# Attention passes of a graph network: one wide addition of keys and values on VectorE, and every fourth step's values added by GpSimd

## Chip, cores and metric

One core of one Trainium2 chip. The metric is the device time of one execution in microseconds (us). The kernel before takes 4827.84 us, the median of 3 runs (4825.83 to 4828.0).

## What is computed

The reference is a residual network over a graph of 6250 nodes with 256 features and 100000 edges, sorted by destination, each with a source, a weight and 194 attributes. First a weighted sum of neighbours with two products and a layer norm, then two attention layers one after the other, a residual and a layer norm. All is float32. The attention layer, twice:

```python
q, k, v = x @ Wq + bq, x @ Wk + bk, x @ Wv + bv       # [n, 4 heads, 64]
e = edge_attr @ We                                     # [edges, 4, 64]
kj, vj = k[src] + e, v[src] + e
logits = einsum('ehc,ehc->eh', q[dst], kj) / sqrt(64)
a = softmax of logits over the edges of one dst
out = segment_sum(vj * a[:, :, None], dst).reshape(n, 256) + x @ Ws + bs
```

What matters here is the line of `kj` and `vj`: the same edge row `e` is added to the gathered key row and to the gathered value row.

## The kernel before

The edges are cut into tiles of 128. Since a tile may touch two or more blocks of 128 destination nodes, each pair of a tile and a block is a step: there are 832, padded. Both attention layers run `edge_pass_attention` (L1130), called as `e1` at L1596 and `e2` at L1599; between them and around them stand short passes over the 49 blocks of nodes. The first also computes a product per block beside its edges (`skip`), the second doesn't. The loops are unrolled; the order on each engine is as written, and semaphores join the engines.

A step `i` of an attention pass:
- GpSimd gathers, for each of the 128 edges, one row of 512 numbers, key and value side by side, from a table in memory into slot `i % 6` of `kv` (L1303, an indirect DMA). It may do so when VectorE has made the value sum of step `i - 6` (`vj_done`). Once in four steps, ahead of the gather of a step with `i % 4 == 2`, it also makes `pick` for the four steps of that quad (L1294, 128x512): a matrix of ones and zeros with which TensorE copies query rows to edges.
- The edge row: in three steps of four TensorE multiplies the edge attributes by `We` (L1315, L1316) into one of two PSUM banks. In the fourth (`i % 4 == 3`) the row comes from a table in memory that the first pass of the program has made; SyncE loads it into `made`, two buffers, when VectorE is done with the quad two before (L1240).
- TensorE: the query rows of the step's edges (L1325).
- VectorE (`logits`, L1403): the key sum into one of two places of `kvj` (L1416), the value sum into one of 44 further places of the same tile (L1420), then for each head a product with the query row and its sum over 64 columns (L1428, an instruction and the reading of its accumulator).
- Every 26 steps are a batch. VectorE, TensorE and ScalarE turn its logits into weights, in stages laid among the steps of the next batch.
- 42 steps behind (`LAG`), ScalarE makes a mask of the step's destinations (L1561, L1567) and multiplies the values by their weights (L1571), 4 instructions; TensorE multiplies mask and weighed values (L1366); VectorE adds the result to the running sums `acc` (L1510). In the last 42 steps VectorE does part of ScalarE's share (L1515, L1517).

A key place is free when the dot products of two steps before are done. A value place is free when ScalarE has weighed the step 44 before it (`weighed`). GpSimd fills all of `kvj` with ones once per pass (L1296), since the last column of each head must be 1; VectorE waits for that before it starts.

Lines that the change and the prediction touch: the load of `made` (L1240), GpSimd's loop (L1296 to L1305), the wait ahead of the edge product (L1314), VectorE's two additions (L1416, L1420) with their waits, and the two places that read values (L1517, L1571).

Of the kernel before, what the change touches and what calls it, by code (L numbers as in the profile page):

```python
# [7 lines left out]
P = 128  # L8
D = 256
H = 4  # L10
C = D // H
# [4 lines left out]
QUAD = 4  # L16
# [1113 lines left out]
def edge_pass_attention(nc, name, k, t, s, w_edge, edge_rows_made, kv_rows, pens, locals16, singles, skip_of):  # L1130
# [13 lines left out]
    with Phase(nc, name) as ph:  # L1144
# [17 lines left out]
        if skip_of is not None:  # L1162
# [21 lines left out]
        made_got = ph.sems("made_got", 2)  # L1184
        w_got, cleared, ones_set = ph.sem("w_got"), ph.sem("cleared"), ph.sem("ones_set")
        e_done, q_done, kj_done, vj_done, dots_done, picked, apart_done = (
            ph.sem(n) for n in ("e_done", "q_done", "kj_done", "vj_done", "dots_done", "picked", "apart_done"))
# [37 lines left out]
        with nc.Block() as block:  # L1225

            @block.sync
            def _(e):
# [9 lines left out]
                def load_made(c):  # L1238
                    if c >= 2:
                        e.wait_ge(vj_done, (c - 1) * QUAD)  # L1240
                    e.dma_start(made[:, c % 2, :], edge_rows_made[c * P:(c + 1) * P, :]).then_inc(made_got[c % 2], 16)
# [45 lines left out]
            @block.gpsimd  # L1287
            def _(e):
                def pick_rows(c):

                    e.wait_ge(spots_got[c % 2], 16 * (c // 2 + 1))
                    if c >= 2:
                        e.wait_ge(q_done, (c - 1) * QUAD)
                    e.tensor_scalar(pick[:, c % 2, :], spots[:, c % 2, :], k["own"][:, 0:1], None, ALU.is_equal).then_inc(picked, 1)  # L1294

                e.memset(kvj[:], 1.0).then_inc(ones_set, 1)  # L1296
                for i in range(T):
                    u = i % NG
                    if i % QUAD == 2:
                        pick_rows(i // QUAD)  # L1300
                    if i >= NG:
                        e.wait_ge(vj_done, i - NG + 1)
                    e.indirect_dma_start(out=kv[:, u, :], out_offset=None,  # L1303
                                         **rows_of(kv_rows, k["src"][:, i:i + 1])).then_inc(kv_got[u], 16)
                e.wait_ge(ones_set, 1)  # L1305

            @block.tensor
            def _(e):
                chosen = Numbers(e, f"{name}_chosen", k["q_row"], (s.blocks - 1) * D)

                def edge_product(a):
                    e.wait_ge(ea_got[a % NE], 16 * (a // NE + 1))
                    if a >= 2:
                        e.wait_ge(vj_done, step_of(a - 2) + 1)  # L1314
                    e.matmul(pe_e[a % 2][:, 0:D], ea[:, a % NE, 0:P], we[:, 0, :], start=True, stop=False)  # L1315
                    e.matmul(pe_e[a % 2][:, 0:D], ea[:, a % NE, P:2 * P], we[:, 1, :],  # L1316
                             start=False, stop=True).then_inc(e_done, 1)
# [74 lines left out]
            def _(e):  # L1392
# [10 lines left out]
                def logits(i):  # L1403
                    j, r = i // BATCH, i % BATCH + 1
                    e.wait_ge(kv_got[i % NG], 16 * (i // NG + 1))
                    c, at = i // QUAD, i % QUAD
# [7 lines left out]
                    if i >= 2:  # L1414
                        e.wait_ge(dots_done, i - 1)
                    e.tensor_tensor(kvj[:, i % 2, :, 0:C], kv[:, i % NG, 0:D].rearrange("p (h c) -> p h c", h=H), edge,  # L1416
                                    ALU.add).then_inc(kj_done, 1)
                    if i >= NV:
                        e.wait_ge(weighed, i - NV + 1)
                    e.tensor_tensor(kvj[:, 2 + i % NV, :, 0:C], kv[:, i % NG, D:].rearrange("p (h c) -> p h c", h=H), edge,  # L1420
                                    ALU.add).then_inc(vj_done, 1)
                    e.wait_ge(kj_done, i + 1)
# [89 lines left out]
                def late_part(n):  # L1512
# [3 lines left out]
                    e.wait_ge(ex_done, b + 1)  # L1516
                    e.tensor_scalar(vals[:, n % R, h * HV:(h + 1) * HV], kvj[:, 2 + n % NV, h, :], ex[:, b % 2, h, r:r + 1], None,  # L1517
# [18 lines left out]
            def _(e):  # L1536
                for i in range(END):
# [18 lines left out]
                    if 0 <= n < T:  # L1556
# [12 lines left out]
                        e.wait_ge(ex_done, b + 1)  # L1569
                        for h in range(H if n < LATE else H - 1):  # L1570
# [83 lines left out]
```

## Time and profile before

| what | us |
|---|---|
| median of 3 runs | 4827.84 |
| profiled execution, device time | 4832.06 |
| its span, first to last instruction | 4830.3 |
| VectorE busy | 3989.0 |
| TensorE matmul busy | 4189.2 |
| ScalarE busy | 2982.2 |
| GpSimd busy | 3116.4 |

Two stretches of the span, 1365 to 2950 us and 3126 to 4690 us, are the two attention passes. Before them lie the making of index tables and the pass of weighted sums. Busy times are unions over an engine's instructions and say nothing yet on who waits for whom; where one instruction's row overlaps the next one's, the distance from start to start is what it costs. The time that an engine is not busy before an instruction is printed with what ended it; "issue" there means that nothing which the profile shows was waited for.

### The profile page before, as it was taken

The page shows a single profiled execution, that of the slowest core. Times are in us where ns is not written, and L with a number is a line of the kernel's source. Part 1 is how long each engine was busy: PE and PEld are TensorE (multiplying, and loading weights), DVE is VectorE, ACT ScalarE, POOL GpSimd, SP SyncE. Part 2 cuts the span into 40 slices and gives each one's busy share as a digit, 9 for nine tenths or more (in the row PEclk, how much of TensorE's full clock was granted, in tenths as well). Part 3 has the DMA queues.
Part 4 walks back from the last instruction along what each step waited for, and adds up shares of the span by engine and source line. Part 5 has one row for each costly group of instructions (what it writes and reads, how often), then busy time and mean ns, then how long its engine had stood idle before and what let it go on. Part 6 is the DMA issues. An engine that isn't in the chain of part 4 may idle for free. (4 is left out here: it accounts for less than half of the span.)

```text
span 4830.3 us, 107746 instructions
## 1 busy us (share of the span) xinstructions
PE 4189.2 (87%) x17694; PEld 3210.6 (66%) x17694; DVE 3989.0 (83%) x22772; ACT 2982.2 (62%) x10607; POOL 3116.4 (65%) x2996
## 2 busy tenths in 40 slices
PE   2887887888979999999999998889999999999988
PEld 2766666675547777777777774567777777777755
DVE  4655555556869999999999998789999999999986
ACT  1111111112319898989898984149999999989971
POOL 6677777740067777777777771287777777777730
PEclk9999999999999999999999999999999999999989
DMA  4666666654568887878788773587777777777734
GB/s 121 189 192 196 192 193 193 191 167 149 169 212 237 233 236 232 233 229 236 231 234 228 231 230 104 173 247 231 226 230 228 231 228 227 226 228 231 226 114 149
DMA packets 663064, 996.73 MB, mean 206 GB/s; under 512 B 99667, under 2 KB 489690, under 8 KB 662407
## 3 DMA queue, kind: packets, MB, share of 16 engines
q0 software_dynamic: 171408, 540.40, 38.1%
q1 hardware_dynamic: 491000, 449.44, 30.8%
q14 instruction: 471, 3.86, 0.3%
q8 instruction: 185, 3.03, 0.3%
HBM read 870.01 MB, written 119.44 MB: 205 GB/s over the span
## 5 line engine op out<-in xcount | busy, mean ns | idle before, releaser
L1303 POOL DMA_INDIRECT e_kv<-kv,src x1664 | 1635.0, 983 | 748.1 <-DVE e_kvj L1420 449.7
L1571 ACT ACTIVATE e_vals<-e_kvj,e_ex 128x65 f32<-128x65 f32 x6572 | 1725.1, 334 | 5.5 <-PE e_sum L1366 5.1
L1366 PE MATMUL e_sum<-e_vals,e_mask 128*128 128x260 f32 x3328 | 1063.7, 403 | 206.2 <-ACT e_vals L1571 190.0
L1325 PE MATMUL e_q<-q,e_pick 128*128 x3328 | 1017.2, 387 | 95.3 <-DVE e_logit L1428 66.4
L1428 DVE CUSTOM_DVE_ANT_0 e_kvj<-e_kvj,e_q 128x64 f32<-128x64 f32 x6656 | 1060.2, 214 | 3.4 <-PE e_q L1325 2.2
L152 POOL DMA_INDIRECT e_x<-x_rows,e_src x783 | 747.3, 954 | 263.1 <-issue 172.3
L1366 PEld LDWEIGHTS e_sum<-e_vals,e_mask 128*128 128x128 f32 x3328 | 563.0, 190 | 454.4 <-issue 379.7
L1325 PEld LDWEIGHTS e_q<-q,e_pick 128*128 128x128 f32 x3328 | 618.2, 191 | 252.4 <-issue 169.9
L1315 PE MATMUL e_e<-e_we,e_ea 112*128 112x256 f32 x2496 | 752.3, 382 | 17.4 <-DMA e_ea<-attr_tiles 16.2
L1316 PE MATMUL e_e<-e_we,e_ea 112*128 112x256 f32 x2496 | 745.8, 380 | 0.0
L1510 DVE TENSOR_TENSOR acc<-acc,e_sum 128x260 f32 x1664 | 697.3, 419 | 41.4 <-issue 23.6
L530 ACT ACTIVATE q<-e_edges 128x512 f32<-128x512 f32 x208 | 124.2, 597 | 925.5 <-PE e_edges L523 921.7
L1294 POOL TENSOR_SCALAR e_pick<-e_spots,own 128x512 f32<-128x512 bf16 x416 | 660.9, 1589 | 15.4 <-DMA e_spots<-locals 1.1
L1567 ACT ACTIVATE e_mask<-e_apart,one 128x128 f32<-128x128 f32 x1580 | 634.6, 402 | 52.5
L597 PE MATMUL e_sum<-e_x,e_mask 128*128 x1664 | 455.2, 400 | 210.6 <-DVE e_mask L612 114.0
L620 DVE TENSOR_TENSOR acc<-acc,e_sum 128x256 f32 x832 | 349.9, 421 | 332.0 <-PE e_sum L597 308.0
L1561 ACT ACTIVATE e_apart<-iota,local 128x128 f32<-128x128 f32 x1580 | 610.4, 386 | 0.0
L1416 DVE TENSOR_TENSOR e_kvj<-e_kv,e_e 128x256 f32<-128x256 f32 x1248 | 513.4, 411 | 66.2 <-DMA e_kv<-kv,src 40.3
L1315 PEld LDWEIGHTS e_e<-e_we,e_ea 112*128 112x128 f32 x2496 | 477.7, 192 | 96.4 <-issue 20.3
L1420 DVE TENSOR_TENSOR e_kvj<-e_kv,e_e 128x256 f32<-128x256 f32 x1248 | 514.7, 412 | 21.0 <-ACT e_vals L1571 20.6
L1428 DVE DVE_READ_ACCUMULATOR2_ANT e_logit<- 128x1 f32 x6656 | 531.6, 80 | 0.2 <-issue 0.2
L597 PEld LDWEIGHTS e_sum<-e_x,e_mask 128*128 128x128 f32 x1664 | 316.9, 198 | 312.2 <-issue 270.2
(223 smaller groups left out, 4479.1 us busy)
## 6 DMA issues: line engine op xcount, KB each, us to landing
e_ea<-attr_tiles SPq DMA_DIRECT2D x1248, 112.0 KB
edges<-q SPq DMA_DIRECT2D x208, 256.0 KB
e_spots<-locals SPq DMA_DIRECT2D x416, 128.0 KB
e_made<-edges SPq DMA_DIRECT2D x416, 128.0 KB
e_kv<-kv,src POOLq DMA_INDIRECT x1664
kv<-n_proj_rows SPq DMA_DIRECT2D x98, 256.0 KB
q<-attr_tiles SPq DMA_DIRECT2D x208, 112.0 KB
n_x<-x_rows SPq DMA_DIRECT2D x98, 128.0 KB
```

What stands on the lines that cost most here:

```text
L152: e.indirect_dma_start(out=self.x[:, at:at + D], out_offset=None, **rows_of(self.t["x_rows"], self.src[:, i:i + 1])).then_inc(self.got[i / ...
L597: e.matmul(sums[i % SUMS][:, 0:D], mask[:, i % R, :], rows, start=True, stop=True).then_inc(summed, 1)
L1294: e.tensor_scalar(pick[:, c % 2, :], spots[:, c % 2, :], k["own"][:, 0:1], None, ALU.is_equal).then_inc(picked, 1)
L1303: e.indirect_dma_start(out=kv[:, u, :], out_offset=None, **rows_of(kv_rows, k["src"][:, i:i + 1])).then_inc(kv_got[u], 16)
L1315: e.matmul(pe_e[a % 2][:, 0:D], ea[:, a % NE, 0:P], we[:, 0, :], start=True, stop=False)
L1316: e.matmul(pe_e[a % 2][:, 0:D], ea[:, a % NE, P:2 * P], we[:, 1, :], start=False, stop=True).then_inc(e_done, 1)
L1325: e.matmul(pe_q[i % 2][:, 0:D], pick[:, c, at:at + P], rows, start=True, stop=True).then_inc(q_done, 1)
L1366: e.matmul(sums[n % 2][:, 0:VALS], mask[:, n % R, :], vals[:, n % R, :], start=True, stop=True).then_inc(summed, 1)
L1428: dot = e.tensor_tensor_reduce(kvj[:, i % 2, h, 0:C], kvj[:, i % 2, h, 0:C], pe_q[i % 2][:, hs], 1.0, 0.0, ALU.mult, ALU.add, logit[:, j % ...
L1510: e.tensor_tensor(rows, rows, sums[n % 2][:, 0:VALS], ALU.add).then_inc(added, 1)
L1567: e.activation(mask[:, n % R, :], apart[:], ACT.Relu, bias=k["one"][:, 0:1], scale=-1.0).then_inc(masked, 1)
L1571: by_weight = e.activation(vals[:, n % R, h * HV:(h + 1) * HV], kvj[:, 2 + n % NV, h, :], ACT.Copy, scale=ex[:, b % 2, h, r:r + 1])
```

## The change

The key sum and the value sum of a step become one VectorE instruction of 512 columns, in three steps of four. It writes to two places of `kvj`, and reads the edge row twice. In the fourth step VectorE makes the key sum alone, and GpSimd makes the value sum from `kv` and `made`, right behind the gather that lies four steps ahead. One semaphore, `kvj_done`, takes the part of `kj_done` and `vj_done`; `values_done` counts GpSimd's sums, one a quad. It is waited for by the gather that overwrites such a slot, by the load of `made`, and by those who weigh such values. The wait for the fill with ones moves from the end of GpSimd's loop ahead of it.

```diff
                 def load_made(c):
                     if c >= 2:
-                        e.wait_ge(vj_done, (c - 1) * QUAD)
+                        e.wait_ge(kvj_done, (c - 1) * QUAD)
+                        e.wait_ge(values_done, c - 1)
...
+                def gather(i):
+                    u = i % NG
+                    if i >= NG:
+                        e.wait_ge(kvj_done, i - NG + 1)
+                        if (i - NG) % QUAD == QUAD - 1:
+                            e.wait_ge(values_done, (i - NG) // QUAD + 1)
+                    e.indirect_dma_start(out=kv[:, u, :], out_offset=None,
+                                         **rows_of(kv_rows, k["src"][:, i:i + 1])).then_inc(kv_got[u], 16)
+
+                def last_values(c):
+
+                    i = QUAD * c + QUAD - 1
+                    e.wait_ge(kv_got[i % NG], 16 * (i // NG + 1))
+                    e.wait_ge(made_got[c % 2], 16 * (c // 2 + 1))
+                    if i >= NV:
+                        e.wait_ge(weighed, i - NV + 1)
+                    by_head = "p (h c) -> p h c"
+                    e.tensor_tensor(kvj[:, 2 + i % NV, :, 0:C], kv[:, i % NG, D:].rearrange(by_head, h=H),
+                                    made[:, c % 2, :].rearrange(by_head, h=H), ALU.add).then_inc(values_done, 1)
+
                 e.memset(kvj[:], 1.0).then_inc(ones_set, 1)
+                e.wait_ge(ones_set, 1)
                 for i in range(T):
-                    u = i % NG
                     if i % QUAD == 2:
                         pick_rows(i // QUAD)
-                    if i >= NG:
-                        e.wait_ge(vj_done, i - NG + 1)
-                    e.indirect_dma_start(out=kv[:, u, :], out_offset=None,
-                                         **rows_of(kv_rows, k["src"][:, i:i + 1])).then_inc(kv_got[u], 16)
-                e.wait_ge(ones_set, 1)
+                    gather(i)
+                    if i % QUAD == QUAD - 1 and i >= QUAD:
+                        last_values(i // QUAD - 1)
+                last_values(s.quads - 1)
...
                 def edge_product(a):
                     e.wait_ge(ea_got[a % NE], 16 * (a // NE + 1))
                     if a >= 2:
-                        e.wait_ge(vj_done, step_of(a - 2) + 1)
+                        e.wait_ge(kvj_done, step_of(a - 2) + 1)
...
                 def logits(i):
...
+                    key_at, value_at = i % 2, 2 + i % NV
...
                     if i >= 2:
                         e.wait_ge(dots_done, i - 1)
-                    e.tensor_tensor(kvj[:, i % 2, :, 0:C], kv[:, i % NG, 0:D].rearrange("p (h c) -> p h c", h=H), edge,
-                                    ALU.add).then_inc(kj_done, 1)
-                    if i >= NV:
-                        e.wait_ge(weighed, i - NV + 1)
-                    e.tensor_tensor(kvj[:, 2 + i % NV, :, 0:C], kv[:, i % NG, D:].rearrange("p (h c) -> p h c", h=H), edge,
-                                    ALU.add).then_inc(vj_done, 1)
-                    e.wait_ge(kj_done, i + 1)
+                    if at < QUAD - 1:
+                        if i >= NV:
+                            e.wait_ge(weighed, i - NV + 1)
+                        e.tensor_tensor(kvj[:, key_at:value_at + 1:value_at - key_at, :, 0:C],
+                                        kv[:, i % NG, :].rearrange("p (a h c) -> p a h c", a=2, h=H),
+                                        edge.unsqueeze(1).to_broadcast([P, 2, H, C]), ALU.add).then_inc(kvj_done, 1)
+                    else:
+                        e.tensor_tensor(kvj[:, key_at, :, 0:C], kv[:, i % NG, 0:D].rearrange("p (h c) -> p h c", h=H), edge,
+                                        ALU.add).then_inc(kvj_done, 1)
+                    e.wait_ge(kvj_done, i + 1)
                     e.wait_ge(q_done, i + 1)
...
# ahead of the values' weighing, in late_part (VectorE) and in ScalarE's loop:
+                    if n % QUAD == QUAD - 1:
+                        e.wait_ge(values_done, n // QUAD + 1)
```

## Rows read from the trace of the kernel before

**Rows 1.** The page's first part: busy us (share of the span) and instructions.

```profile
PE 4189.2 (87%) x17694; PEld 3210.6 (66%) x17694; DVE 3989.0 (83%) x22772; ACT 2982.2 (62%) x10607; POOL 3116.4 (65%) x2996
```

**Rows 2.** Windows of both attention passes: start:end length, then each engine's busy us.

```profile
1365.00:2915.00 1550.00, 1409.39 (x6225) 1117.64 (x6226) 1460.25 (x9656) 1330.36 (x4848) 1147.53 (x1041) 0.99 0.80 232
3126.00:4647.00 1521.00, 1377.42 (x6036) 1081.30 (x6037) 1448.25 (x9611) 1328.83 (x4848) 1148.47 (x1041) 0.99 0.77 229
```

**Rows 3.** Waits, 3400 to 4500 us: waiting instruction, releaser, total us, times, longest.

```profile
POOL e_kv L1303 <- DVE e_kvj L1420: 163.8, 222, 3.2
PE e_sum L1366 <- ACT e_vals L1571: 75.5, 128, 1.7
ACT e_lr L1546 <- DVE e_lr L1474: 53.2, 23, 3.3
```

**Rows 4.** Timeline of POOL, filling phase: start us, duration us, instruction, idle before it.

```profile
1354.96 10.06 POOL L1296 MEMSET e_kvj<- 128x11960 f32 x1 [19.43 <-POOLq L81]
...
1367.43 1.59 POOL L1294 TENSOR_SCALAR e_pick<-e_spots,own 128x512 f32<-128x512 bf16 x1
1369.19 1.03 POOL L1303 DMA_INDIRECT e_kv<-kv,src  x1 [0.17 <-issue]
...
1371.79 0.96 POOL L1303 DMA_INDIRECT e_kv<-kv,src  x1 [0.30 <-issue]
1373.05 0.96 POOL L1303 DMA_INDIRECT e_kv<-kv,src  x1 [0.30 <-issue]
1374.04 1.59 POOL L1294 TENSOR_SCALAR e_pick<-e_spots,own 128x512 f32<-128x512 bf16 x1
```

**Rows 5.** The gathers' line in each pass: durations min/median/max ns, first and last start.

```profile
L1303 POOL DMA_INDIRECT e_kv<-kv,src x832: 942/955/1524, 1365.2 to 2908.6; - x167
L1303 POOL DMA_INDIRECT e_kv<-kv,src x832: 942/955/1403, 3126.3 to 4640.0; - x167
```

**Rows 6.** Timeline of DVE in a stretch without softmax work.

```profile
3615.88 0.40 DVE L1416 TENSOR_TENSOR e_kvj<-e_kv,e_e 128x256 f32<-128x256 f32 x1
3616.21 0.40 DVE L1420 TENSOR_TENSOR e_kvj<-e_kv,e_e 128x256 f32<-128x256 f32 x1
3616.54 0.20 DVE L1428 CUSTOM_DVE_ANT_0 e_kvj<-e_kvj,e_q 128x64 f32<-128x64 f32 x1
...
3617.45 0.40 DVE L1416 TENSOR_TENSOR e_kvj<-e_kv,e_e 128x256 f32<-128x256 f32 x1
```

**Rows 7.** Timeline of DVE: a scan that waits for the copy ahead of it.

```profile
3613.39 0.24 DVE L1458 COPY e_row_b<-e_small 1x104 f32<-1x104 f32 x1
3613.67 0.41 DVE L1460 TENSOR_TENSOR_SCAN e_out_f<-e_over,e_row_f 1x128 f32<-1x128 f32 x1
```

**Rows 8.** The line of a DVE addition of 512 columns, one operand in PSUM.

```profile
L744 DVE TENSOR_TENSOR n_proj_rows<-n_proj,n_b_proj x98: 658/691/692, 1125.6 to 3112.1; 128x512 f32<-128x512 f32 x98
```

**Rows 9.** Groups by form, POOL: busy us, mean ns of one | idle before.

```profile
L984 POOL MEMSET acc<- 128x260 f32 x49 | 15.4, 315 | 181.0 <-DVE n_rows L947 181.0
```

**Rows 10.** DVE in the first filling phase: its waits (1366 to 1445 us), and one start.

```profile
DVE e_kvj L1416 <- DMA e_kv<-kv,src: 23.3, 13, 12.0
...
1374.73 0.42 DVE L1416 TENSOR_TENSOR e_kvj<-e_kv,e_e 128x256 f32<-128x256 f32 x1 [1.00 <-issue]
```

**Rows 11.** Timeline: three scans of DVE, each with the pick beside it.

```profile
1510.99 1.59 POOL L1294 TENSOR_SCALAR e_pick<-e_spots,own 128x512 f32<-128x512 bf16 x1
1511.26 0.72 DVE L1433 TENSOR_TENSOR_SCAN e_fw<-e_pen,e_lr 128x128 f32<-128x128 f32 x1
...
4225.07 1.60 POOL L1294 TENSOR_SCALAR e_pick<-e_spots,own 128x512 f32<-128x512 bf16 x1
...
4225.78 0.42 DVE L1433 TENSOR_TENSOR_SCAN e_fw<-e_pen,e_lr 128x128 f32<-128x128 f32 x1
...
4321.59 0.98 DVE L1433 TENSOR_TENSOR_SCAN e_fw<-e_pen,e_lr 128x128 f32<-128x128 f32 x1
...
4322.22 1.74 POOL L1294 TENSOR_SCALAR e_pick<-e_spots,own 128x512 f32<-128x512 bf16 x1
```

More of the change, by code:

```diff
@@ L1183, in edge_pass_attention @@
             ph.sems("kv_got", NG), ph.sems("ea_got", NE), ph.sems("runs_got", 2), ph.sems("spots_got", 2))
-        made_got = ph.sems("made_got", 2)
+        made_got, values_done = ph.sems("made_got", 2), ph.sem("values_done")
         w_got, cleared, ones_set = ph.sem("w_got"), ph.sem("cleared"), ph.sem("ones_set")
-        e_done, q_done, kj_done, vj_done, dots_done, picked, apart_done = (
-            ph.sem(n) for n in ("e_done", "q_done", "kj_done", "vj_done", "dots_done", "picked", "apart_done"))
+        e_done, q_done, kvj_done, dots_done, picked, apart_done = (
+            ph.sem(n) for n in ("e_done", "q_done", "kvj_done", "dots_done", "picked", "apart_done"))
         flat_done, lr_done, fw_done, mx_inner = (ph.sem(n) for n in ("flat_done", "lr_done", "fw_done", "mx_inner"))
@@ L1569, in _ @@
                         e.wait_ge(ex_done, b + 1)
+                        if n % QUAD == QUAD - 1:
+                            e.wait_ge(values_done, n // QUAD + 1)
                         for h in range(H if n < LATE else H - 1):
```

## Prediction

> **What bounds the kernel now.** I read the page's summary first: TensorE (PE), VectorE (DVE), ScalarE (ACT) and GpSimd (POOL) are busy for 87, 83, 62 and 65% of the span [rows 1], and such shares decide nothing, since the change touches only the two attention stages. So second the busy time by stage, from the first to the last step of each attention pass: in both, DVE is busy for 94 to 95%, PE for 91%, ACT for 86 to 87%, POOL for 74 to 76% [rows 2]. DVE is the nearest to full. The reader should then ask what the others wait for. Over 1100 us of the second pass ACT stops mainly once a batch, 53.2 us in 23 waits, for DVE's L1474; PE's largest wait is for ACT's weighed values; POOL's is for DVE to free a slot of gathered rows, 163.8 us [rows 3]. DVE thus sets the pace, but none of the three others is far off. ACT alone could give back no more than about 5%. And POOL looks idle for a quarter, but that reading is wrong: between two gathers of 0.95 us that wait for nobody there are 0.30 us in which nothing is recorded (1373.05 to 1374.04 with a pick behind it, 1367.43 to 1374.04 for a whole cycle), so four gathers and one pick cost POOL 6.61 us from pick to pick when nobody holds it [rows 4]. The passes have 832 steps, that is 208 groups of four ("quads"), and their gathers span 2908.6 - 1365.2 = 1543.4 us and 4640.0 - 3126.3 = 1513.7 us [rows 5]: 7.43 and 7.29 us for each of 207.75 quads. POOL's real slack is only 0.82 and 0.68 us a quad.
>
> **DVE, part by part.** In a stretch without softmax work one step takes 1.57 us from key addition to key addition; the key addition starts 0.33 us before the value addition, that one 0.33 us before the first dot product (3615.88, 3616.21, 3616.54: 0.66 us in all), though each lasts 0.40 [rows 6]. So two instructions that don't wait for each other overlap by 0.07 us. One that waits for the instruction just ahead doesn't: the copy at 3613.39 lasts 0.24, and the scan that needs it starts at 3613.67, 0.04 us after its end [rows 7].
> - Three steps of four: two additions of 256 columns become one of 512. The row of an addition of 512 columns with one operand in PSUM has 691 ns as its median [rows 8]. Its result is needed at once by the dot product, with nothing in between any more, so the dots start after 0.69 + 0.04 = 0.73 us in place of 0.66: 0.07 us *later*. The wide addition is no gain; bounds are 0.66 (the shortest of that row) and 0.82 (two of the old ones added up, if the repeated operand or the jump between the two results costs something). I take 0.71 with its wait, as the narrow ones here run nearer to 0.40 than 0.42: 0.05 us later.
> - The fourth step: the value addition leaves DVE. The dots start after 0.40 + 0.04 = 0.44 in place of 0.66: 0.22 us saved.
> - A quad: 0.22 - 3 x 0.05 = 0.07 us saved, 14 us in the 197 quads of a pass behind its filling phase; with the bounds of the wide addition between 0.10 saved (20 us) and 0.38 lost (75 us).
>
> **POOL.** It gets 416 additions of 128x256 with two SBUF operands. There is no such row. From below: a memset of 260 columns takes 315 ns and one of 11960 takes 10.06 us [rows 4, 9], that is 0.098 + 0.000833 a column, 0.31 us for 256. From above: the pick's 1.59 us, whole. In between: three streams one behind the other by the memset's slope give 0.74 us, two (the write beside the reads) 0.52, and the pick's rate for half its columns 0.79. I take 0.70, nearer to the three streams and the pick's rate. The pick shows that an instruction put between gathers costs its own duration and no more: 6.61 - 4 x 1.26 (1373.05 - 1371.79) = 1.57 [rows 4]. A quad costs POOL 6.61 + 0.70 = 7.31 us, a pass 207.75 x 7.31 = 1518.7 us, against gathers that now span 1543.4 and 1513.7. POOL's floor therefore lies 25 us below the first pass and **5 us above the second**.
> - The filling phase: until ACT and the sums start, some 42 steps, DVE has less to do and is the one that waits for gathered rows, 23.3 us in 13 waits [rows 10]. Here POOL is the pace and each quad gets the full 0.70: 10.5 x 0.70 = 7 us more in each pass.
> - Waits added on POOL: the new addition stands behind the gather four steps on, and waits for that step's rows (landed: a gather's rows are there 4.5 us after it, 1369.19 + 1.03 against 1374.73 [rows 4, 10]), for the table's rows, and for ACT to have weighed the step that used the slot 44 steps ago. Behind it stand all further gathers and the next pick, and behind the pick PE's queries. When POOL leads, this wait would eat lead only; when POOL is late, as I expect, ACT is through. Nothing as such; up to 5 us a pass for the coupling of two engines that are equally full go to the range. The memset's wait ahead of the loop costs below 0.2 us. The wait on SP, ahead of the load of the table's rows, holds up later loads of edge attributes, which are requested four products ahead: nothing.
> - Waits on ACT and DVE for the POOL result come 42 steps later: nothing.
>
> **Contention.** DVE operations with two SBUF operands can be held up by POOL. A scan that usually lasts 0.42 took 0.72 us when a pick had started 0.27 before it, and 0.98 when one started 0.63 after it, and that pick took 1.74; one that started 0.71 us into a pick took its usual 0.42 [rows 11]. By the durations, 16 of the 320 scans and subtractions of this sort (L1433, L1436, L1474) are longer by 0.3 to 0.57; the rows named are the first and the last of L1433's eight. The changed kernel has a POOL instruction that reads two tiles, and one DVE addition a quad with two SBUF operands. At that rate, 5% of 208 + 160 operations by 0.4 us is 7 us a pass; bounds are 0 and, at one collision in every second quad, 42. I take 6.
> Beside this row: the Trainium skill (SBUF — State Buffer, Who interferes with whom) says that a DVE instruction with two SBUF inputs and a GpSimd instruction that reads SBUF exclude each other for the whole instruction. The trace agrees in part: it shows the hold-up, but not for the whole 1.59 us of a pick.
>
> **The sum**, against the profiled execution (4832.06 us, span 4830.3; the median of the runs is 4827.84, 4.2 less). First pass: DVE stays the pace, -14 + 7 + 6 = -1 us. Second pass: by DVE 1513.7 - 1 = 1512.7, by POOL 1518.7; the larger holds, +5 us. Together +4. 
>
> **Rivals.**
> - *POOL's addition is cheap and DVE's relief stands.* At 0.5 us, near the two streams, POOL's floor is 1477 and binds nowhere; without collisions each pass gets -14 + 5 = -9 us, and with a wide addition at its lower bound -15. Time 4810, down to 4798. For it: ACT and PE have some 5% to give [rows 3]. Against: the pick's rate.
> - *POOL becomes the bound of both passes.* It decides from 0.67 us (second pass) and 0.81 us (first) on. At 0.90 the floor is 207.75 x 7.51 = 1560: +17 and +47, time 4892; at 0.80, 1539: +0 and +26, time 4854. For it: POOL's slack, and that a strided result and three waits may cost more than a memset. It would show as DVE and PE waiting for gathers and picks.
> - *Exclusion hits the quads regularly*, since the new addition starts near DVE's key addition of the same step, both being released by the same progress: every second quad by 0.4 us, 42 us a pass in place of 6: +36 in the first pass and, over POOL's floor, +30 in the second, time 4898.
> - *The wide addition costs what two did.* 0.82 + 0.04: 75 us lost in place of 14 saved, in the first pass 89 more and over POOL's floor 83 in the second: 5004. Against it: the row of 512 columns.
>
> **How the numbers follow.** Forecast 0.42, cheap addition 0.25, POOL-bound 0.23, exclusion 0.06, wide addition 0.04. Break-even for the whole is a POOL addition of about 0.68 us. Range 4803 to 4885: it takes in most of the cheap case and the POOL-bound one up to 0.88 us. Faster by over 0.2%: most of the cheap case and a little of the forecast, 0.28. Slower: the last three and the forecast's upper edge, 0.40. Within: 0.32.
>
> **What would show it.** POOL's cycle in the filling phase: 7.3 us from pick to pick. The wide addition: 0.68 to 0.69 us, and the first dot product 0.03 to 0.04 us behind its end. DVE's busy share falls by some 3 points in both passes, POOL's waits for DVE shrink to a few us, and the wait of DVE or PE for gathers and picks appears in the second pass. The first pass should be within 5 us of before, the second a little longer. I am wrong if POOL's addition is outside 0.60 to 0.80 us, or if the dots start behind the wide addition without the gap.

## The result, and the profile after

The changed kernel takes **4924.51 us** (median of 4 runs, 4915.34 to 4935.86) against 4826.84 us of the kernel before beside it (4818.96 to 4828.0): ratio 1.0207, 95% interval 1.0178 to 1.0236. It is 98 us slower; I had said 4832, within 4803 to 4885. The attention passes, from the first gather to the last sum, grew from 1595.9 and 1567.0 to 1648.4 and 1612.8 us; all else moved by 2 us.

The page's first part, to be set beside [rows 1], and the windows of both passes, beside [rows 2]:

```profile
PE 4213.2 (85%) x17694; PEld 3202.5 (65%) x17694; DVE 4003.5 (81%) x21108; ACT 2995.0 (61%) x10607; POOL 3465.7 (70%) x3412
```

```profile
1367.00:2971.00 1604.00, 1426.72 (x6231) 1118.26 (x6232) 1474.95 (x8836) 1338.48 (x4854) 1320.88 (x1248) 0.99 0.77 225
3182.00:4752.00 1570.00, 1391.84 (x6039) 1080.66 (x6040) 1451.95 (x8790) 1336.65 (x4854) 1323.19 (x1248) 0.99 0.75 221
```

DVE executes 1664 instructions fewer and is busy for *longer*: 1474.95 and 1451.95 us in place of 1460.25 and 1448.25. Its share fell from 95 to 92% only because the passes are longer. POOL has 174 us more a pass, of which 208 x 0.74 = 154 would be additions that nobody disturbs.

The steps of the prediction one by one. POOL's timeline in the filling phase, beside [rows 4]:

```profile
1383.22 1.58 POOL L1295 TENSOR_SCALAR e_pick<-e_spots,own 128x512 f32<-128x512 bf16 x1
1384.98 1.04 POOL L1303 DMA_INDIRECT e_kv<-kv,src  x1 [0.17 <-issue]
1386.32 0.95 POOL L1303 DMA_INDIRECT e_kv<-kv,src  x1 [0.31 <-DVE e_kvj L1440]
1387.29 0.74 POOL L1314 TENSOR_TENSOR e_kvj<-e_kv,e_made 128x256 f32<-128x256 f32 x1
1388.19 0.96 POOL L1303 DMA_INDIRECT e_kv<-kv,src  x1 [0.16 <-POOL e_kvj L1314]
1389.46 0.96 POOL L1303 DMA_INDIRECT e_kv<-kv,src  x1 [0.30 <-PE e_q L1345]
1390.45 1.59 POOL L1295 TENSOR_SCALAR e_pick<-e_spots,own 128x512 f32<-128x512 bf16 x1
```

The addition takes 0.74 us, and from pick to pick it is 7.23 us: I had 0.70 and 7.3. DVE in a quiet stretch, beside [rows 6]; the four dot products of each step are left out but for the first:

```profile
3640.28 0.42 DVE L1444 TENSOR_TENSOR e_kvj<-e_kv,e_made 128x256 f32<-128x256 f32 x1
3640.73 0.22 DVE L1452 CUSTOM_DVE_ANT_0 e_kvj<-e_kvj,e_q 128x64 f32<-128x64 f32 x1
...
3641.30 0.42 DVE L1534 TENSOR_TENSOR acc<-acc,e_sum 128x260 f32 x1
3641.64 0.68 DVE L1440 TENSOR_TENSOR e_kvj<-e_kv,e_e 128x512 f32<-128x512 f32 x1
3642.36 0.22 DVE L1452 CUSTOM_DVE_ANT_0 e_kvj<-e_kvj,e_q 128x64 f32<-128x64 f32 x1
...
```

The fourth step lasts 1.36 us (3640.28 to 3641.64; forecast 1.57 - 0.22 = 1.35), and the dots start 0.72 us after a wide addition starts (forecast 0.71). Alone, each instruction costs what I said. What is different stands in three other views. First the groups of the whole execution (line, engine, operation, tiles, shapes, count | busy us, mean ns | idle before, its releasers), of before and then of after; scans and scalings stand for the softmax's instructions:

```profile
L1416 DVE TENSOR_TENSOR e_kvj<-e_kv,e_made 128x256 f32<-128x256 f32 x416 | 171.1, 411 | 6.1 <-DMA e_kv<-kv,src 5.7
L1436 DVE TENSOR_TENSOR_SCAN e_mx<-e_pen,e_ends,e_fw 128x128 f32<-128x128 f32 x64 | 31.0, 484 | 2.3
L1485 DVE TENSOR_SCALAR e_scale<-e_scale,goes_on 1x4 f32<-1x4 f32 x64 | 16.5, 257 | 2.2
L1420 DVE TENSOR_TENSOR e_kvj<-e_kv,e_e 128x256 f32<-128x256 f32 x1248 | 514.7, 412 | 21.0 <-ACT e_vals L1571 20.6
```

```profile
L1444 DVE TENSOR_TENSOR e_kvj<-e_kv,e_made 128x256 f32<-128x256 f32 x416 | 212.5, 511 | 4.5 <-DMA e_kv<-kv,src 4.1
L1460 DVE TENSOR_TENSOR_SCAN e_mx<-e_pen,e_ends,e_fw 128x128 f32<-128x128 f32 x64 | 36.5, 570 | 2.3
L1509 DVE TENSOR_SCALAR e_scale<-e_scale,goes_on 1x4 f32<-1x4 f32 x64 | 27.8, 435 | 2.2
L1314 POOL TENSOR_TENSOR e_kvj<-e_kv,e_made 128x256 f32<-128x256 f32 x416 | 334.0, 803 | 90.4 <-ACT e_vals L1599 81.5
L1440 DVE TENSOR_TENSOR e_kvj<-e_kv,e_e 128x512 f32<-128x512 f32 x1248 | 848.1, 680 | 142.3 <-ACT e_vals L1599 82.2 <-DMA e_kv<-kv,src 50.4 <-PE e_e L1336 4.9
```

The fourth step's key addition is 0.10 us longer in the mean, 41.4 us in all; the softmax's scans, scalings and subtraction (636 instructions in both passes) went from 249.7 to 293.3 us, another 43.6. Together 85 us where I had taken 12. POOL's addition is not beside all of these: 134 of the 636 ran beside it and took 31 us more than the medians of before, and 186 beside a pick took 21 us more, where 166 had taken 5. The last two rows show the second thing: POOL stands for 81.5 us (60 waits) before its addition, and DVE for 82.2 us before its wide one, and both wait for ACT, for the weighing that frees a value's place. DVE's value addition of before (L1420) had waited 20.6 us for it, POOL never.

How a long key addition comes about, in the timeline of both engines, at two places:

```profile
1672.72 1.44 DVE L1444 TENSOR_TENSOR e_kvj<-e_kv,e_made 128x256 f32<-128x256 f32 x1
1673.12 0.74 POOL L1314 TENSOR_TENSOR e_kvj<-e_kv,e_made 128x256 f32<-128x256 f32 x1
...
1674.19 0.22 DVE L1452 CUSTOM_DVE_ANT_0 e_kvj<-e_kvj,e_q 128x64 f32<-128x64 f32 x1
...
3415.61 1.01 DVE L1444 TENSOR_TENSOR e_kvj<-e_kv,e_made 128x256 f32<-128x256 f32 x1
3416.22 0.98 POOL L1314 TENSOR_TENSOR e_kvj<-e_kv,e_made 128x256 f32<-128x256 f32 x1
```

At the second place the key addition would by its usual 0.41 us have ended at 3416.02, 0.20 us before POOL's recorded start, and took 1.01 all the same: the recorded starts don't tell which of the two held up the other. Of the 416 key additions 135 took over 0.44 us, 90 of them over 0.60; of the 133 that took over 0.45, 127 had POOL's addition beside them, each time that of the same step. 121 of POOL's additions took over 0.78. The third view is the waits of 3400 to 4500 us, beside [rows 3]; the first line is of the kernel before:

```profile
DVE e_kvj L1420 <- ACT e_vals L1571: 8.7, 42, 0.3
```

```profile
ACT e_lr L1572 <- DVE e_lr L1498: 73.6, 23, 4.2
PE e_sum L1386 <- ACT e_vals L1599: 73.5, 98, 2.0
DVE e_kvj L1440 <- ACT e_vals L1599: 34.4, 68, 0.8
PE e_q L1345 <- DVE e_logit L1452: 30.1, 38, 1.4
POOL e_kv L1303 <- DVE e_kvj L1440: 20.1, 71, 2.3
POOL e_kvj L1314 <- ACT e_vals L1599: 14.6, 16, 2.0
```

Over these 1100 us ACT waits 20 us longer for DVE's subtraction, which comes once a batch (23 waits), and DVE and POOL wait 49 us for ACT's weighed values, where DVE had waited 8.7. I call this the ring: engines that wait for each other in turn, though none of them is full.

### The profile page after: what moved, and what is told of

It is laid out like the page before. It is cut to its first block and busy times, and to the rows that moved or that the text cites. A ratio compares the mean times of both kernels' runs of the same rounds, so it can differ in the third digit from the quotient of the medians.

```text
span 4930.5 us, 109334 instructions
## 1 busy us (share of the span) xinstructions
PE 4213.2 (85%) x17694; PEld 3202.5 (65%) x17694; DVE 4003.5 (81%) x21108; ACT 2995.0 (61%) x10607; POOL 3465.7 (70%) x3412
## 5 line engine op out<-in xcount | busy, mean ns | idle before, releaser
L1345 PE MATMUL e_q<-q,e_pick 128*128 x3328 | 1030.9, 391 | 152.0 <-DVE e_logit L1452 105.8
L1452 DVE CUSTOM_DVE_ANT_0 e_kvj<-e_kvj,e_q 128x64 f32<-128x64 f32 x6656 | 1075.9, 218 | 61.6 <-PE e_q L1345 3.9
L1440 DVE TENSOR_TENSOR e_kvj<-e_kv,e_e 128x512 f32<-128x512 f32 x1248 | 848.1, 680 | 142.3 <-ACT e_vals L1599 82.2
L1452 DVE DVE_READ_ACCUMULATOR2_ANT e_logit<- 128x1 f32 x6656 | 547.8, 82 | 0.2 <-issue 0.2
L1335 PEld LDWEIGHTS e_e<-e_we,e_ea 112*128 112x128 f32 x2496 | 479.8, 193 | 92.5 <-issue 17.7
L1336 PEld LDWEIGHTS e_e<-e_we,e_ea 112*128 112x128 f32 x2496 | 474.3, 190 | 71.1
```

The costliest lines, as they stand in the source:

```text
L1345: e.matmul(pe_q[i % 2][:, 0:D], pick[:, c, at:at + P], rows, start=True, stop=True).then_inc(q_done, 1)
L1440: e.tensor_tensor(kvj[:, key_at:value_at + 1:value_at - key_at, :, 0:C], kv[:, i % NG, :].rearrange("p (a h c) -> p a h c", a=2, h=H), edg ...
L1452: dot = e.tensor_tensor_reduce(kvj[:, i % 2, h, 0:C], kvj[:, i % 2, h, 0:C], pe_q[i % 2][:, hs], 1.0, 0.0, ALU.mult, ALU.add, logit[:, j % ...
```

## The experiments

Times are compared as ratios to the kernel before on the same chip; 0.0010 is 4.8 us. One thing must be said first: on two of the chips, 10 and 14, things differ. There the kernel before takes 5127 to 5155 us, some 300 more. On chip 14, 210 of them lie ahead of the attention, and each attention pass is 45 us longer, with short stalls in it. I first give the kernels measured where the kernel before takes 4824 to 4828 us, as in the first comparison (chips 2, 5 and 9).

**The wide addition alone** (from before; nothing on POOL):

```diff
+ if at < QUAD - 1:   # three steps of four
+     e.tensor_tensor(kvj[:, key_at:value_at + 1:value_at - key_at, :, 0:C], ... to_broadcast([P, 2, H, C]), ALU.add)
+ else:               # as before
+     two additions of 256 columns
```

> The kernel before with the wide addition in three steps of four and the two narrow ones in the fourth, nothing on GpSimd; ahead of it the ratio was 1.0083 on a chip where the kernel before takes 5155 us. Theory A (the wide addition gives up the overlap of two narrow ones and makes DVE's value addition wait for ScalarE before the key addition too, +30 to +40 us beside the loss of 0.05 us a step, 60 in all): on a chip where the kernel before takes 4824 to 4828, ratio 1.007 to 1.014 (+34 to +68 us), with the idle time ahead of the wide addition grown to over 1.2 us a batch. Theory B (my prediction's sizes): 0.05 us by 3 x 197 steps in two passes, +59 less what slack hides, but without any growth of the waits for ScalarE; ratio up to 1.012. The two differ in the waits, not the time. Theory C (the wide addition costs nothing by itself, all of the loss is GpSimd's): 0.999 to 1.002.

4883.32 us, **1.0122** (1.0107 to 1.0138): +59 us.

```profile
L1420 DVE TENSOR_TENSOR e_kvj<-e_kv,e_e 128x512 f32<-128x512 f32 x1248 | 847.4, 679 | 112.3 <-ACT e_vals L1580 62.0 <-DMA e_kv<-kv,src 36.2 <-PE e_e L1316 7.4
```

My 0.05 us a step gives 3 x 197 x 2 x 0.05 = 59 us. But 62 us of waits for ACT are here too, in place of 20.6, so the agreement in the sum is partly luck and doesn't show that the arithmetic is all of it. Theory C, that the wide addition is harmless, is out.

**The changed kernel without POOL's addition** (every fourth step's values lack the sum):

```diff
- e.tensor_tensor(kvj[:, 2 + i % NV, :, 0:C], kv[...], made[...], ALU.add).then_inc(values_done, 1)
```

> The changed kernel without GpSimd's addition, so every fourth step's values lack the sum; ratio was 1.0013 on the chip where the kernel before takes 5155. Theory A (DVE relieved by 0.33 us in a fourth step and slower by 0.05 in the three others comes out near nothing, since ScalarE and DVE wait for each other at each batch): 1.000 to 1.005 on a chip where before takes 4824 to 4828. Rival (GpSimd's addition costs nothing but the collisions, 58 us): the fills in its place gave 1.0084, so without it 1.007 to 1.009. Second rival (DVE sets the pace as predicted, -14 us a pass): 0.994.

4841.34 us, **1.0032** (1.0021 to 1.0043): +15 us. DVE alone, relieved as the change relieves it and with nothing to disturb it, is no faster: the fourth step gives back 59 - 15 = 44 us of the 87 that I had counted.

```profile
L1431 DVE TENSOR_TENSOR e_kvj<-e_kv,e_e 128x512 f32<-128x512 f32 x1248 | 848.2, 680 | 142.3 <-ACT e_vals L1586 84.1 <-DMA e_kv<-kv,src 41.8 <-PE e_e L1327 11.4
L1435 DVE TENSOR_TENSOR e_kvj<-e_kv,e_made 128x256 f32<-128x256 f32 x416 | 171.4, 412 | 4.5 <-DMA e_kv<-kv,src 4.5
```

The key addition is back at 412 ns, and the wait for ACT stays at 84.1 us.

**POOL's addition replaced by two fills**, of 0.30 and 0.33 us, that read nothing in SBUF, with all its waits (each fourth step's values are ones, not sums):

```diff
- e.tensor_tensor(kvj[...], kv[...], made[...], ALU.add).then_inc(values_done, 1)
+ e.memset(filler[:], 1.0)                                  # 224 columns
+ e.memset(kvj[:, 2 + i % NV, :, 0:C], 1.0).then_inc(values_done, 1)
```

> The changed kernel in which GpSimd, in place of the addition, fills the step's value place and a spare tile of 224 columns with ones: 0.31 + 0.29 us on GpSimd at the same place with the same waits, but no operand read from SBUF, so that these values are wrong. Theory A (GpSimd's reading of two operands holds up VectorE's two-operand instructions, 1.5 us a batch): VectorE's key addition of the fourth step is back at 0.41 us from 0.52, the scans at 0.45 to 0.48, and the time 40 to 90 us below the changed kernel. Rival C (GpSimd's time and its wait for ScalarE): within 20 us of the changed kernel.

4863.52 us, **1.0084** (1.0067 to 1.0101): +41 us.

```profile
L1446 DVE TENSOR_TENSOR e_kvj<-e_kv,e_made 128x256 f32<-128x256 f32 x416 | 171.9, 413 | 3.2 <-DMA e_kv<-kv,src 2.9
```

The whole change is at 1.0207, 59 us (0.0123) more (the key additions are normal here, and the softmax's instructions take 258.5 us in place of 293.3). POOL's time and waits are the 0.0052 over the kernel without them, 25 us. The fills are shorter, though: their cycle from pick to pick in the filling phase is 6.99 us (1379.73 to 1386.72) against 7.23, so a part of the 59 may be length and not reading. The next run has nearly the length and all of the reading.

**POOL's reading alone**: the kernel before, with an addition of 224 columns and two SBUF operands into a tile that nobody reads; DVE's work is untouched and POOL never waits for ACT:

```diff
+ e.tensor_tensor(filler[:], kv[:, i % NG, D:]...[:, :, 0:56], made[:, c % 2, :]...[:, :, 0:56], ALU.add)
```

> The kernel before with an addition of 224 columns with two SBUF operands every fourth gather on GpSimd, whose result nobody reads; DVE's work is unchanged. Theory A (collisions in SBUF cost some 58 us of the 97, as the fills in place of the addition showed, and GpSimd's time costs a little more): ratio 1.010 to 1.016 on a chip where the kernel before takes 4824 to 4828, with the scans and the fourth step's key and value additions longer. Rival (collisions need the changed order on DVE, since the fourth step's key addition and GpSimd's addition start near each other only there): 1.000 to 1.005.

4888.45 us, **1.0133** (1.0117 to 1.0149): +64 us.

```profile
L1433 DVE TENSOR_TENSOR e_kvj<-e_kv,e_made 128x256 f32<-128x256 f32 x416 | 196.2, 472 | 3.4 <-DMA e_kv<-kv,src 3.0
L1437 DVE TENSOR_TENSOR e_kvj<-e_kv,e_made 128x256 f32<-128x256 f32 x416 | 200.9, 483 | 0.0
```

The two additions with SBUF operands are longer by 25.1 and 28.0 us, the softmax's by 27.4: 80 us of DVE's time. How much of the 64 us is this and how much POOL's longer cycle, the run doesn't separate. Those with an operand in PSUM stay at 410 and 411 ns. So the collisions need neither the wide addition nor the new order.

**POOL's part with narrow additions on DVE** in the three other steps:

```diff
- e.tensor_tensor(kvj[:, key_at:value_at + 1:value_at - key_at, ...], ...)
+ e.tensor_tensor(kvj[:, key_at, ...]) ; e.wait_ge(weighed, ...) ; e.tensor_tensor(kvj[:, value_at, ...])
```

> The variant with narrow additions in three steps of four and GpSimd's addition in the fourth once more. On its first chip it was 1.2% faster than before, where the kernel before itself was slower in its attention passes than on the chip of the first comparison. If this is a chip of that kind, 0.988 again. If it is like the first one (before 4827 us), theory A: the change's 98 us less some 70 for the wide addition, so 1.003 to 1.010; rival B (the wide addition is all of the loss): 0.990.

4858.5 us, **1.0072** (1.0054 to 1.0089). The better half of the change, and still a loss of 35 us. Against it the wide addition costs 0.0135, 65 us.

**The ring, by the room in it.** NV = LAG + 2 leaves two steps between the dot products and the weighing. LAG = 40 and NV = 44 leave four, with the same memory:

```diff
- LAG = BATCH + 8 * PACE
- NV, NG, NE, R = LAG + 2, 6, 5, 4
+ LAG = BATCH + 7 * PACE
+ NV, NG, NE, R = LAG + 4, 6, 5, 4
```

> The kernel before with the weighing following the dot products by 40 steps in place of 42, and 44 places for values as before, so four steps of room in place of two. Theory (the coupling of DVE and ScalarE by this room costs time in the kernel before too): on a chip where the kernel before takes 4824 to 4828, 0.995 to 0.998, which beats both kernels. Rival (what is not waited for there comes back as the wait for the softmax and the scale, as the kernel with both, 1.0066 against 1.0072 without, suggests): 0.998 to 1.002.

> The changed kernel with the weighing following the dot products by 40 steps in place of 42 (44 places for values as before): four steps of room between VectorE and ScalarE in place of two. Theory A (VectorE's 82 us of waits for ScalarE's weighed values, which the change brought, are a real part of the 97 us): on a chip where the kernel before takes 4824 to 4828, ratio 1.010 to 1.015. Rival (the waits only show where ScalarE or the softmax chain sets the pace, and come back elsewhere once the room is there, as in the kernel before, 1.0012 with that room): 1.017 to 1.022.

> The changed kernel without GpSimd's addition (every fourth step's values lack the sum), with the same four steps of room; with two steps it gave 1.0032. Theory A (the relief of 0.22 us in each fourth step was half lost in VectorE's waits for ScalarE, 84 us here): 0.993 to 0.998 on a chip where the kernel before takes 4824 to 4828. Rival (the time between two batches is set by the loop of softmax, ScalarE's weighing and the sums, whatever the room): 1.001 to 1.004.

| kernel | two steps of room | four steps |
|---|---|---|
| before | 1 | 1.0012 (1.0003 to 1.002) |
| without POOL's addition | 1.0032 (1.0021 to 1.0043) | 1.0006 (0.9995 to 1.0018) |
| whole change | 1.0207 (1.0178 to 1.0236) | 1.0092 (1.007 to 1.0114) |
| POOL's part, narrow additions | 1.0072 (1.0054 to 1.0089) | 1.0066 (1.0049 to 1.0083) |

```profile
DVE e_kvj L1440 <- DMA e_kv<-kv,src: 52.0, 36, 12.1
DVE e_scale L1519 <- ACT e_scale L1580: 26.0, 41, 2.0
...
POOL e_kv L1303 <- DVE e_kvj L1440: 103.2, 222, 2.6
```

These are waits of the changed kernel with four steps, over both passes; the lines of DVE's L1440 and POOL's L1314 waiting for ACT are gone, and 26.0 us of another wait for ACT have come (the edit also brings the weighing two steps nearer to the softmax that it needs). The whole change gets 0.0115, 56 us, back (theory A expected less), and POOL's addition costs 0.0086 (42 us) in place of 0.0175 (84 us). Not all of this need be waiting, for the collisions are fewer too:

```profile
L1444 DVE TENSOR_TENSOR e_kvj<-e_kv,e_made 128x256 f32<-128x256 f32 x416 | 197.3, 474 | 3.8 <-DMA e_kv<-kv,src 3.2
```

The key additions take 197.3 us in place of 212.5 and the softmax's instructions 275.4 in place of 293.2, together 33 us less of DVE's time. How the 56 us divide between the waits and these 33 isn't shown. The kernel before loses its 20.6 us of waits and gains nothing, and DVE's part goes from +15 to +3 us, not to -10 to -34: here the rival is nearly right, the waits come back elsewhere. The narrow kernel with four steps:

> Narrow additions in three steps of four, GpSimd's addition in the fourth, and the weighing 40 steps behind over 44 places. Both theories: below the variant without the last of these, by 20 to 40 us (the waits for ScalarE that it still has), so on a chip of the second kind 0.982 of before, on one of the first kind 0.995 to 1.003.

1.0066 against 1.0072: it gains nothing, unlike the whole change, though its key additions and softmax instructions too take 25 us less of DVE's time. Both theories had expected 20 to 40 us. Why the edit helps only together with the wide addition and POOL's I haven't tested.

**The wide addition with its bubble filled**, in all four steps, the addition of the sums put between it and the dot products; nothing on POOL:

```diff
- logits(i); late_part(...); add_sums(...)
+ sums_of(i); late_part(...); add_sums(...); dots(i)
```

> The kernel before with the wide addition in all four steps and nothing on GpSimd, and with the addition to the running sums placed between the wide addition and the dot products that need it. Theory A (a wide addition of 0.68 us is worth 0.08 us, and loses 0.12 because nothing stands between it and its reader): now a step costs 0.61 + 0.34 + 0.57 = 1.52 us in place of 1.57, 1.3 us a batch: 40 to 80 us below before, if the chip has no stalls of its own. Rival D (VectorE and ScalarE wait for each other in turn, so that VectorE's relief in quiet steps is lost): within 20 us of before.

4840.96 us, **1.0033** (1.0021 to 1.0046).

```profile
L1431 DVE CUSTOM_DVE_ANT_0 e_kvj<-e_kvj,e_q 128x64 f32<-128x64 f32 x6656 | 1065.0, 215 | 7.8 <-PE e_q L1325 2.6 <-issue 0.3
L1419 DVE TENSOR_TENSOR e_kvj<-e_kv,e_e 128x512 f32<-128x512 f32 x1248 | 848.3, 680 | 130.8 <-ACT e_vals L1576 84.0 <-DMA e_kv<-kv,src 41.1 <-issue 2.2
```

DVE stands for 7.8 us before its dots, where with the wide addition alone it stood for 46.8. It is no gain over before, and theory A's 40 to 80 us didn't come: the kernel is slower by 16 us, where the wide addition alone lost 59, and a relief of DVE again goes with a wait for ACT (84.0 us).

**On the other kind of chip.** First the two kernels themselves:

> The kernel before itself, unchanged, for its trace on the chip on which the others of this call run. In the last call a kernel before of 5155 us stood beside four variants, 328 us above its first chip, of which the pass of weighted sums took 216 in their traces. Theory A: the rest, 112 us, lies in the attention passes, which then are slower on such a chip for this kernel more than for those with a busier GpSimd. Rival: the rest lies elsewhere. If the chip is like the first one, 4827 us.

> The changed kernel itself, for its trace and its ratio on this chip. If the chip is like the first: 1.02 times before. If it is like the second one: theory A (GpSimd's addition costs, the chip doesn't matter) 1.02 again; rival B (on such a chip the delay of the gathers is no loss, as the two variants with that addition were 0.8 and 1.2% faster there) 0.995 to 1.005.

5130.78 (1.0004, 0.999 to 1.0019) and 5134.01 us (**1.002**, 1.0008 to 1.0032): there the change costs 10 us (4 to 16). The passes of the changed kernel, 1645.9 and 1615.0 us, are what they were in the first comparison; those of the kernel before are longer, 1641.3 and 1612.0. Its dot products are idle for 60.9 us in place of 3.4:

```profile
L1428 DVE CUSTOM_DVE_ANT_0 e_kvj<-e_kvj,e_q 128x64 f32<-128x64 f32 x6656 | 1060.2, 213 | 60.9 <-DVE e_kvj L1416 48.9 <-DMA e_spots<-locals 3.5 <-PE e_q L1325 2.2
```

An engine is named as the releaser that had long been done. The stalls come near the ends of batches, and in the kernels with an addition on POOL the dots have next to none of them. What they are I can't say. Four more kernels there, on chip 10:

> The kernel before with the wide addition alone: three steps of four add keys and values in one VectorE instruction of 512 columns, the fourth keeps its two narrow ones, GpSimd gets nothing. Theory A (VectorE's own sum is near zero, and the loss of the change comes from GpSimd's addition): the dots start 0.05 us later in 1248 steps, 62 us at most; some of it falls into waits, so 4870 to 4890 us. Rival B (the wide addition is the whole loss): 4920 us or more. Rival C (only GpSimd's time counts): 4827 us.

> The changed kernel with two narrow additions in three steps of four; GpSimd still makes the values of the fourth. Theory A: VectorE gets back 0.05 us in 1248 steps, 30 to 60 us below the changed kernel's 4924: 4865 to 4895 us, slower than before although VectorE does strictly less, since GpSimd's addition holds up VectorE's operations with two SBUF operands. Rival B (wide addition guilty): 4800 us, faster than before. Rival C (GpSimd's time is the bound): as the changed kernel, 4915 to 4930.

> The changed kernel with GpSimd's addition left out, so that the value sums of every fourth step are not made. Theory A: what is left is VectorE's own sum, 0.07 us a quad saved, 0 to 25 us below before: 4800 to 4830 us. Rival B (the wide addition is the loss): 4900 us or more. Rival C (GpSimd's time alone): also 4800 to 4830, so this run tells only B apart.

> The kernel before, in which GpSimd additionally makes an addition of 224 columns of the fourth step's values and the table's rows into a tile that nobody reads, at the place where the change has it; VectorE is unchanged, and there is no wait for ScalarE. Its price on GpSimd is 0.65 us. Theory A (collisions plus filling phase): slower by 50 to 90 us, 4880 to 4915, with VectorE's key addition of the fourth step and the scans lengthened. Rival B (wide addition guilty): 4827 to 4845. Rival C (GpSimd's cycle alone, 6.61 + 0.65 = 7.26 us a quad): 4830 to 4850, VectorE's rows as before.

They gave 1.0083 (1.0064 to 1.0101), 0.9878 (0.9861 to 0.9894), 1.0013 (1.0003 to 1.0023) and 0.9923 (0.9906 to 0.9939). Read by themselves they say that work on POOL makes the kernel *faster*; on the chips of the first comparison the same four are at 1.0122, 1.0072, 1.0032 and 1.0133. The wide addition is a loss on both. With more room, on chip 14:

> The changed kernel with the weighing 40 steps behind in place of 42, over the same 44 value places: VectorE, and GpSimd's addition, may run four steps ahead of ScalarE in place of two. Theory A (VectorE and ScalarE wait for each other in turn: ScalarE for the softmax's subtraction once a batch, 3.5 us, then VectorE and GpSimd for ScalarE's weighing, 1.6 and 0.8 us a batch, because the room between them is two steps): 1.5 us a batch less, 60 to 90 us below the changed kernel. Rival B (collisions of operands in SBUF are all of the loss): within 20 us of the changed kernel.

> The kernel before with the same room: weighing 40 steps behind over 44 places. Its waits for ScalarE are 0.4 us a batch. Theory A: 0.4 to 1 us a batch less, 25 to 60 us below before. Rival B: within 10 us of before.

0.9937 (0.9917 to 0.9957) for the changed kernel and 0.9968 (0.9955 to 0.9981) for the one before. Where the first comparison ran, nothing that I tried beats the kernel before.

## Why the prediction was wrong

The sum again, with what the runs give, in us over both passes (measured: differences of ratios times 4827, each uncertain by some 7 to 10, those with the whole change by 14 to 16, and taken on several chips of the first kind):

| term | predicted | measured | from |
|---|---|---|---|
| wide addition in three steps | +59 | +59 | wide alone |
| fourth step's value addition off DVE | -87 | -44 | without POOL's addition, less wide alone |
| POOL's time and its waits | +20 | +25 | fills, less without POOL's addition |
| collisions in SBUF | +12 | +59, with what the fills are shorter | whole change, less fills |
| sum | +4 | +99 | |

- **Right**: DVE's sizes (0.68 and the gap, 0.22 saved a fourth step), POOL's addition (0.74 us alone, just the three streams by the memset's slope; 0.70 taken, 0.60 to 0.80 allowed), its cycle, the overlap that a dependent instruction loses, and that DVE's work hardly shrinks. "I am wrong if POOL's addition is outside 0.60 to 0.80 us, or if the dots start behind the wide addition without the gap" named the wrong doubts. In the mean the addition took 0.803 us, because it is held up as well. The estimate of 0.66 us that the prediction draws from the Trainium skill (GPSIMD Engine Reference, Performance versus the Vector engine) is a slip: by its 4497 ns for 2048 columns, 256 columns would, as an estimate, be 0.56 us, further below the 0.74 measured.
- **Right by luck**: +20 for POOL. It was made of 14 for the filling phase and 6 for a floor of POOL over the second pass; that floor, 7.23 x 207.75 = 1502 us, lies below DVE's 1512.7 and binds nowhere, and POOL waits 81.5 us for ACT, which the sum didn't have.
- **Wrong, the mis-sized term**: "At that rate, 5% of 208 + 160 operations by 0.4 us is 7 us a pass; bounds are 0 and, at one collision in every second quad, 42. I take 6." DVE lost 85 us, 43 a pass; by the experiments about 30 a pass reach the end. The rate was that of the pick, whose place in the order is another. A fourth step's key addition and POOL's addition belong to the same step, and 127 of 416 met. The gathered rows, for which both wait, did not bring them together: before none of these 127 did either engine stand waiting for rows, and 13 of POOL's came behind a wait for ACT. What keeps the two engines so near to each other no run shows. The rival "Exclusion hits the quads regularly" comes nearest (42 a pass, 4898 us); I gave it 0.06. Its 42 are nearly the 43 measured, but by luck: it had only the key additions, every second by 0.4 us, which gave 21, and the softmax's instructions gave the other 22. Of those the scans and the subtraction had been in the 5%, at too low a rate, and the scalings of 1x4 (257 to 435 ns) not at all. Beside the rows: the Trainium skill (SBUF — State Buffer, Who interferes with whom) has the two exclude each other for the whole instruction, and the key addition at 1672.72 agrees: 1.44 us, of which POOL's whole 0.74. That whichever starts first has the ports (the Trainium skill, the same page, SBUF: two separate sides) does not fit there by the records: DVE's started 0.40 us ahead, and POOL's was not held.
- **Wrong, the waits**: "Nothing as such; up to 5 us a pass for the coupling of two engines that are equally full go to the range." "when POOL is late, as I expect, ACT is through" was wrong: POOL's wait for ACT is 81.5 us, and all later gathers stand behind it. "DVE stays the pace, -14 + 7 + 6 = -1 us" took DVE's relief as whole; with nothing on POOL it brought 44 of 87. ACT stops at each softmax until DVE's subtraction is there, DVE then stops until ACT has weighed; a step of DVE that is shorter between two softmaxes only reaches the next wait sooner, as I read it; that is argued, not shown. Four steps of room brought the whole change 56 us, fewer collisions included, but without POOL's addition only 13 of the missing 43: there the rival stands, that the loop of softmax, weighing and sums sets the time of a batch whatever the room.
- **The rivals.** POOL as the bound is out: its floor of 1502 us lies under gathers that span 1597.0 and 1562.7 us, shown here beside [rows 5]. The cheap addition is out by 0.74. The wide addition at the price of two is out by its 680 ns.

```profile
L1303 POOL DMA_INDIRECT e_kv<-kv,src x832: 942/964/1824, 1367.1 to 2964.1; - x167
L1303 POOL DMA_INDIRECT e_kv<-kv,src x832: 942/962/1330, 3182.2 to 4744.9; - x167
```

**What stays open**: why only half of DVE's relief reached the end; how the 59 us of collisions and the 25 of POOL's time divide exactly, since the fills are shorter than the addition and the ring makes terms depend on each other (wide alone and reading alone add up to 123, less the 44 of the fourth step to 79, and 99 were measured); what part of the 56 us is the room and what the 33 us of collisions that went with it; and why that edit helps only the whole change.

## What to carry to other kernels

Work moved from VectorE to GpSimd isn't priced by its duration there: count the VectorE instructions with two SBUF operands in the stretch, the softmax's small ones too, and ask whether the moved one runs beside one of them in each round, for the rate of another instruction (here 16 of 320) says nothing of it (127 of 416). When three engines of a loop are over 85% busy and wait for each other once a batch, a saving on the fullest may bring half (44 of 87 us here), and a new wait on an engine that issues the gathers holds up all that comes behind it; look at how many steps of room lie between the engines. Fusing two instructions that overlap bought nothing here, where the result is needed at once: 0.72 us from the start of the wide addition to the dots in place of 0.66.

## What I had not expected of the hardware

- An addition with two SBUF operands on VectorE took 1.44 us in place of 0.41 when GpSimd's addition began 0.40 us after it. Another took 1.01 us though GpSimd's began only after its usual end.
- Chips differ: the kernel before takes 4824 to 4828 us on some and 5127 to 5155 us on others, and the ratio of the same two kernels is 1.0207 on one chip of the first kind and 1.002 on one of the other; for an addition on GpSimd (narrow on VectorE) even the sign turns, 1.0072 against 0.9878.
